# A vision-transformer block with a state-space scan on Trainium2: two VectorE steps and one set of stacked copies issued one or two scans later

## The reference, cut to what matters

```python
proj = einsum('bsd,ed->bse', layernorm(h), in_proj_w); hidden, gate = split(proj)
h = silu(depthwise_conv(hidden, conv_w) + conv_b)
ts, Bm, Cm = split(einsum('bis,ei->bse', h, x_proj_w), [R, R + N])
dt = softplus(einsum('bsr,ir->bsi', ts, dt_proj_w) + dt_proj_b)   # last step times alpha
dA = exp(A * dt); dBu = dt * Bm * h                               # 16 states per channel
state = dA_t * state + dBu_t; y = einsum('bin,bn->bi', state, C_t)
out = einsum(((y + h * D) * silu(gate)), out_proj_w)
```

## Time and profile before

| what | value |
|---|---|
| median of 3 runs | 379.56 us |
| the three runs | 379.56, 376.74, 380.18 us |
| the profiled execution | 368.0 us |
| its span, first to last instruction | 366.3 us |
| its mean granted TensorE clock | 0.956 |
| busy in the span: TensorE, VectorE, ScalarE, GpSimd | 90%, 65%, 53%, 56% |

### The profile page before, as it was taken

The page is one execution under the profiler, slowest core; times in us unless marked ns, Lnnn a source line. Parts: engine busy times, 40 slices in busy tenths (PEclk is TensorE's granted clock), DMA queues, the critical chain, the costliest instruction groups (busy, mean ns, idle before and its releaser), DMA issues.

```text
span 366.3 us, 6306 instructions
## 1 busy us (share of the span) xinstructions
PE 330.1 (90%) x2042; PEld 270.4 (74%) x2043; DVE 239.3 (65%) x365; ACT 194.1 (53%) x331; POOL 204.2 (56%) x162
## 2 busy tenths in 40 slices
PE   5699979999998788799769999989999999999990
PEld 5653756847876676688668988878888888888870
DVE  1366997989998999999997588864332332223320
ACT  1146993957995666685916649952222222222220
POOL 8120287687896999898875327720333333333332
PEclk9999996999999999899979689999999999999997
DMA  7990820000023320410899999262223322222212
GB/s 188 238 329 17 337 123 2 2 1 5 0 113 118 116 115 4 115 45 2 187 199 233 292 215 236 92 140 70 52 51 52 48 45 45 40 47 50 36 21 22
DMA packets 30184, 37.01 MB, mean 101 GB/s; under 512 B 6112, under 2 KB 26128, under 8 KB 29136
## 3 DMA queue, kind: packets, MB, share of 16 engines
q1 hardware_dynamic: 24160, 30.84, 31.6%
q0 software_dynamic: 4080, 4.39, 7.1%
q10 hardware_dynamic: 1920, 1.46, 1.7%
HBM read 28.29 MB, written 8.40 MB: 100 GB/s over the span
## 4 chain that ended last, share of the span: by engine, by line
PE 34%; DMA 22%; DVE 16%; issue 14%; POOL 7%; ACT 5%; POOLq 1%; SPq 0%; DVEq 0%; ACTq 0%
DMA out<-ysb,token_r 17%; DVE decays L1179 7%; PE ps L1740 6%; POOL rows_scratch L691 5%; PE ps L1694 4%; DMA c_all<-in_xT 3%; ACT decays L836 3%; PE ps L1900 2%; PE ps L1503 2%; POOL states L600 2%; DVE ysb L1410 1%; PE ps L1588 1%; DVE hidden L1095 1%; DVE diagB L1084 1%; PE ps L1534 1%
## 5 line engine op out<-in xcount | busy, mean ns | idle before, releaser
L600 POOL TENSOR_TENSOR states<-decays,c_all 128x1024 f32<-128x1024 f32 x48 | 113.9, 2397 | 19.1 <-DVE decays L1179 19.1
L1179 DVE TENSOR_TENSOR_SCAN decays<-decays,ps 128x1024 f32<-128x1024 f32 x48 | 107.5, 2263 | 3.8 <-PE ps L1694 3.2
L703 POOL DMA_INDIRECT out<-ysb,token_r x23 | 36.1, 1570 | 68.7 <-DVE ysb L1410 57.5
L836 ACT ACTIVATE decays<-dt,negA 128x504 f32<-128x504 f32 (+1 forms) x104 | 62.0, 676 | 7.5 <-POOL states L600 7.4
L956 ACT ACTIVATE sa<-ps 128x512 f32<-128x512 f32 x31 | 18.5, 597 | 80.5 <-PE ps L1866 77.7
L1740 PE MATMUL ps<-ident,states 128*128 128x128 f32 x384 | 55.7, 291 | 4.9 <-POOL states L600 3.5
L1740 PEld LDWEIGHTS ps<-ident,states 128*128 128x128 f32 x384 | 44.1, 148 | 8.9 <-POOL states L600 4.1
L1694 PE MATMUL ps<-diagB,stacked_u 64*128 64x128 f32 x384 | 39.8, 302 | 10.8 <-DVE decays L1179 9.2
L1694 PEld LDWEIGHTS ps<-diagB,stacked_u 64*128 64x128 f32 x384 | 29.5, 194 | 25.1 <-DVE decays L1179 14.8
L1900 PE MATMUL ps<-w,hT 128*128 (+1 forms) x248 | 45.4, 326 | 0.8 <-ACT hT L960 0.8
L1900 PEld LDWEIGHTS ps<-w,hT 128*128 128x128 f32 x248 | 41.8, 190 | 3.5 <-issue 1.0
(11 more groups left out here) (210 smaller groups left out, 589.8 us busy)
## 6 DMA issues: line engine op xcount, KB each, us to landing
c_all<-c_scratch SPq DMA_DIRECT2D x8, 1024.0 KB, 4.7
w_raw<-in_w13T SPq DMA_DIRECT2D x9, 512.0 KB, 11.3
w_raw<-in_w13T SPq DMA_DIRECT2D x18, 256.0 KB, 11.4
w<-in_w2T SPq DMA_DIRECT2D x9, 384.0 KB, 15.5
xs<-rows_scratch SPq DMA_DIRECT2D x23, 128.0 KB, 2.1
rows_scratch<-zeros SPq DMA_DIRECT2D x5, 520.0 KB, 6.3
c_all<-in_xT SPq DMA_DIRECT2D x8, 256.0 KB, 10.9
out<-h SPq DMA_DIRECT2D x1, 576.0 KB, 5.5
```

The costliest lines, as they stand in the source:

```text
L600: pool.tensor_tensor(states[:, n % SLOTS, :].rearrange("p (n b s) -> p n b s", n=NH, b=2), decays[:, k % DBUF, t, :, :, :].rearrange("p b ...
L703: pool.indirect_dma_start(out=out_d, out_offset=bass.IndirectOffsetOnAxis(ap=token_r[:, r:r + 1], axis=0), in_=ysb[:, r, :], in_offset=Non ...
L836: return act.activation(decays[:, k % DBUF, tiles[0]:tiles[1], :, n, 1:], dt[g][:, i, tokens].rearrange("p (a b s) -> p a b s", b=2, s=S)[ ...
L1179: dve.tensor_tensor_scan(both, both, unit_banks(n).rearrange("p b n -> p (b n)"), 0.0, ALU.mult, ALU.add).then_inc(scan_ok, 1)
```

## The change

Three engines' hand-written orders are edited; no instruction is added or removed and no tile is changed.

- VectorE: `u_low_part(1)` moves from behind scan 4 (the fifth) to behind scan 5 (the sixth), ahead of `convolved(1, 2)`, which already stood there. `time_step(0, 2)` moves from behind scan 6 to behind scan 7 (the eighth).
- GpSimd: `inputs_of(0, 2)`, which needs that time step, moves from behind `weighted(6)` to behind `weighted(7)`.
- TensorE: `u_copies(1, 0)` moves from behind unit 5 to behind unit 6, and `u_copies(1, 1)` from behind unit 6 to behind unit 7, ahead of `project(6)`.

```diff
@@ GpSimd, behind weighted(n)
-                if n == 6:
+                if n == 7:
                     inputs_of(pool, 0, 2)
@@ VectorE, behind scanned(n)
-                if n == 4:
+                if n == 5:
                     u_low_part(1)
-                if n == 5:
                     convolved(1, 2)
-                if n == 6:
+                if n == 7:
                     time_step(0, 2)
@@ TensorE, behind inputs(n) and summed(n - 3)
-                if n in (5, 13, 22, 28, 37):
-                    u_copies((5, 13, 22, 28, 37).index(n) + 1, 0)
-                if n in (6, 14, 23, 29, 38):
-                    u_copies((6, 14, 23, 29, 38).index(n) + 1, 1)
+                if n in (6, 13, 22, 28, 37):
+                    u_copies((6, 13, 22, 28, 37).index(n) + 1, 0)
+                if n in (7, 14, 23, 29, 38):
+                    u_copies((7, 14, 23, 29, 38).index(n) + 1, 1)
```

## The result

The ratio of the changed kernel to the kernel before came out at 1.0120, with a 95% interval of 1.0070 to 1.0171: slower, where no change was forecast. The medians of all 21 runs of each say something else, 376.63 us against 377.50, a ratio of 0.998; both lie in the stated range of 375.1 to 382.6. The ratio is what comes out if only runs within 1.5% of each kernel's own fastest execution count, for before's fastest is then the profiled one of 368.0 us, two of its 21 runs remain (371.40 and 372.82, median 372.11) against 19 of the changed kernel (median 376.55), and 376.55 / 372.11 = 1.012.

A forecast was written before the change was run, and what follows sets the result against it. All engines are near-busy in the scans, with TensorE setting the pace from 76.40 to 112.00 us. −0.02 us at `inputs(9)` and 0 at scan 10 left 368.0 us profiled; carrying over 11.6 gave 379.5 us, range 375.1 to 382.6.

The forecast's parts named there:

- The low part's lateness: VectorE: the moved low part starts at 66.49 us and ends at 67.18, its wait of 1.01 us gone.
- the hole behind it: TensorE: a new wait of 0.65 us ahead of the first copies, until the low part is ready near 67.2.
- ScalarE's lateness: ScalarE: the `Ln` ends 2.2 us later, at 74.08, swallowed in the 3.76 us wait for the last projection.
- the time step caught behind GpSimd: VectorE: the third time step, ready at 74.08, ends 0.55 us behind GpSimd, at 76.89; scan 8 0.6 us later.
- 0 at scan 10, and the same rows behind it: End of the sum: scan 10 still starts at 81.76 us, paced by TensorE, and everything later is unchanged.
- rows behind unit 12 shifted by more than 0.5 us: Stated sign of being wrong: rows after unit 12 shift by over 0.5 us, where none was forecast.
- the sum of TensorE: TensorE from `inputs(5)`: row spacings added up put `inputs(9)` at 76.39 us against 76.41, so nothing is won.
- the other of the prediction's signs of being wrong: TensorE: `inputs(9)` starts over 0.5 us away from the forecast 76.4 us.
- the clock rival: TensorE's clock falls behind the new wait ahead of the copies: 3.4 us lost, 383.0 us; chance 0.08.
- Rival C: TensorE: slow clock stays or returns behind the new wait ahead of the copies, 383.0 us; chance 0.08.
- A: VectorE: the time step slips in ahead of GpSimd, scan 8 near 74.7; 378.8 us, at most 378.0; chance 0.22.
- B: Moved waits cost more than removed ones if the low part ends after 67.3: 380.2 us, bound 381.9; chance 0.17.

The follow-up runs named there:

- first profile after: The changed kernel's first profiled execution, against the profile of the kernel before: span 374.8 us, 8.5 more; clock full from 54.90 to 64.05 us.
- the second control: The kernel before, unchanged, against itself: 377.80 us (12 runs), ratio 0.9997 (0.9918 to 1.0076); its profile spans 376.1 us.
- the second profile: The changed kernel, unaltered, profiled again on a chip where the kernel before runs at 367.03 us: span 363.1 us.
- The second comparison: The changed kernel again, against the kernel before on the same chip: 365.54 us (12 runs) against 367.03 (31), ratio 0.9962 (0.9934 to 0.9989).

## Why the prediction was right and wrong

**Right: the new waits.** The low part's lateness, the hole behind it, ScalarE's lateness of 2.2 us (2.3 measured) and where it is swallowed, and the time step caught behind GpSimd all stand in the profiles. The two profiles of the changed kernel that, like the one before, ran slow ahead of 64 us are the ones to measure against: in the first of them the time step starts 0.41 us behind scan 7 and takes 2.67, and scan 8 starts 13.69 us behind `inputs(5)` where it was 13.11, the 0.6 us of the forecast. The first profile after agrees as well (76.92 against 76.28), but partly by luck: at full clock throughout, the kernel before has scan 8 at 13.80 us behind `inputs(5)` and the changed one at 13.90. The hole was forecast at 0.65 us; it was 0.44 and 0.33 at slow clock and 1.09 twice at full clock. The Trainium skill, "SBUF — State Buffer", section "Who interferes with whom", has a VectorE instruction with two SBUF inputs contend with a GpSimd instruction that reads SBUF, and the issue order decides which one is blocked. The trace agrees: 2.67 us where GpSimd's unit 7 had started, 0.86 where the time step was ready before it.

**Wrong, and the step on which the forecast of no change failed: "0 at scan 10, and the same rows behind it".** The sum took everything behind scan 10 from one profiled execution of 368.0 us, and carried the 11.6 us up to the timed median over as a constant, of which it said that nothing shown tells where they lie. The rows behind were not the same: they made the profile after 8.5 us longer, by the standing stretch of 11.4 us less 2.9 elsewhere. One of the prediction's own signs of being wrong (rows behind unit 12 shifted by more than 0.5 us) is thereby met. The stretch is not the edit's, for the second control has it at 9.7 us, and it is the size of the 11.6. That the kernel before was profiled without it and timed mostly with it is therefore the likely account; it is not shown, as the timed runs of 371.4 to 382.1 us left no trace. The ratio of 1.012 sets the two fastest of those runs against 19 of the changed kernel. By the medians of all 21 runs the change moved 0.9 us, and the range of 375.1 to 382.6 held.

**Wrong: the sum of TensorE.** It laid `project(7)` (2.07 us) and `inputs(9)` end to end, because in the rows before they stood apart. They stood apart only for the wait. Where none is between them they run into each other, as `project(6)` and `inputs(8)` did in the very rows used: 2.4 us for the pair, not 2.07 + 0.59. So `inputs(9)` starts 12.08 us behind `inputs(5)`, not 13.22 (at 75.29 in the first profile after, not 76.4, which is the other of the prediction's signs of being wrong), and is done 0.3 us sooner. The forecast of 0.0 should have been −0.3: 17.49 against 17.81. In the rows it is always the 64-row half of a projection that is overlapped so, never the 128-row half; whether the row count is the reason was not tested.

**Wrong: one state of the clock.** The sum was made on one profiled execution. At full clock the kernel before has two waits, 0.53 us ahead of the copies and 1.10 ahead of `inputs(9)`, and the change is worth 0.8 us (18.50 − 17.69).

**Wrong: the clock rival sat in the wrong kernel.** Rival C let the clock fall behind the new hole. It stood at 1.00 from the hole to 84 us in all four profiles of the changed kernel, with holes of 0.3 to 1.1 us ahead of the copies. It fell behind the old wait in one of three profiles of the kernel before and when that wait was put back, and cost 1.64 us both times. By the Trainium skill, "TensorE: Matmul & The Clock Gate", Part 1, activity is what releases the slow level; TensorE was busy on both sides of these waits, so the rows neither bear that out nor contradict it, and it gave no reason to look behind the old wait rather than the new. Its Part 4, by which transposes do not count as activity in the same way, made the new order look the riskier one; the trace does not agree. The change takes the old wait out in all four profiles, and with it that risk, which no term of the sum held.

**The other rivals.** A did not come about: the time step was ready 0.2 us too late to get in ahead of unit 7 (73.47, when unit 7 had started at 73.25, in the second profile), and it did get in when it was moved alone. B's condition, a low part done after 67.3, was just met in the first profile after, at 67.31; the hole of 1.09 us is 0.56 more than the one that the kernel before has there at full clock, and less than the wait of 1.10 that is gone.

**The range and the sign.** The gain by the trace is 0.3 to 0.8 us, 0.1 to 0.2%, and more where the clock would have fallen. The second comparison measures 0.4%, 0.1 to 0.7%. What ends the waits of the standing stretch stays open, and so does a part of what the time step alone wins: 3 to 5 us by medians, 1.0 to 1.4 by the trace.

## What to carry to other kernels

Before a profiled execution stands for the timed ones, find out where the two differ: here they lay 11.6 us apart, and one stretch far from the edit takes 9.7 to 11.6 us longer in most executions and not in others. When a wait is taken away, let neighbours on the same engine run into each other in the sum, and look for a pair in the trace that already does. A move that only shifts a wait can still win, if the clock falls behind the old place and not behind the new one, so profile several executions before forecasting. Move one step at a time: here one half of the edit won 1.0 to 1.4 us and the other gave 0.6 to 0.7 of it back.

## What was not expected of the hardware

TensorE's granted clock went to 0.50 about 1 us behind the end of a wait of 0.97 and of one of 1.08 us, though it was busy before and after, and stayed at full level behind waits of 0.76, 0.88 and 1.10 us at the same place in other executions. The same program ran at a median of 367.03 us on one chip and 377.50 to 380.33 on others. In profiles of the kernel before, with spans of 364.5 and 376.1 us, 9.7 of the 11.6 us between them lie in one stretch near 230 us, in which TensorE, VectorE and ScalarE all slacken at once: from 226 to 239 us they are busy for 7.4, 3.8 and 5.5 us with it, and for 13.0, 10.9 and 12.8 without.
